# The D term of a selective scan: from the head of a batch to its second half, two products per state

## Chip, cores and metric

The kernel runs on one NeuronCore of a Trainium2 chip. The metric is the device time of one execution in microseconds (us). Its engines are TensorE (PE; PEld are its weight loads), VectorE (DVE), ScalarE (ACT), GpSimd (POOL) and SyncE (SP), which here only issues DMAs. Each engine works through its own list of instructions in order and waits on semaphores. L12 is line 12 of the kernel.

## What is computed

The whole is a two-layer block on x of 4 batches x 512 tokens x 256 features. The change touches only the state-space scan of its first layer:

```
def step(h, inp):
    dt_t, B_t, C_t, u_t = inp
    dA = jnp.exp(dt_t[:, :, None] * A)
    h = dA * h + (dt_t * u_t)[:, :, None] * B_t[:, None, :]
    y = jnp.einsum('bdn,bn->bd', h, C_t)
    return (h, y)
...
y = ys.transpose(1, 0, 2) + u2 * D
y = y * jax.nn.silu(z)
out = y @ W_out
return x + out
```

d runs over 512 channels, n over 16 states. `u2 * D` is the D term: each channel's input times one number of that channel. It doesn't depend on the state n, so it can be added to y at any point.

## The kernel before

**Stages.** Up to about 320 us the inputs of the scan are made; from there to about 655 us the scan runs; then come the rest of layer 0 and all of layer 1. The order within each engine is written by hand.

**The scan** is a loop over k = 0 to 63, with `b, n = divmod(k, 16)`: batch b, state n. Channels lie on the 128 partitions in M = 4 groups, tokens along the free axis in TILES = 4 tiles of 128. For each k:

- ACT: `times_b(k)` multiplies `duT` (dt*u2, token-major) by the state's column of B (L1716, and a scaled identity, L1717), and `decays(k, h)` makes exp(dt*A) for each half h of the channels (L1728).
- PE: `feed(k, 0)` and `feed(k, 1)` turn these products to channel-major in banks 4 to 7 of PSUM (transposes L996, one product per group L997). Half h of state k needs the scan of that half for k-1 to be done.
- DVE: `scan(k, 0)`, `scan(k, 1)` (L2133), each over 2 channel groups x 512 tokens, from PSUM into one of 7 state buffers. (The listing of instructions names their form SCALAR_TENSOR_TENSOR, the profile TENSOR_TENSOR_SCAN.)
- POOL: multiplies the state by its row of C (L2593).
- PE: `sum_state(j)`, 16 transposes (L1008) that turn the product back to token-major and add it into banks 0 to 3, one bank for each tile of tokens. It runs up to two states behind the scan: after the feeds of state k up to two sums are done, as long as `due <= k - 2`.

**The D term** (`d_term`, L950 to L959) adds u2*D into the same four banks: per tile one bf16 product of zeros, 512 wide, which opens the whole bank (L954, `nought`), and four products of a 128x128 block of `u2` with `diag`, a diagonal matrix of D (L956). In the profile each f32 product and its weight load stand as two records, a transpose as one. For batch 0 all four tiles come before the scan, ahead of the last `turn_du` (L944), which turns `du` of the batch prepared last; ACT copies that to `duT` (L1706).

**The turn of a batch.** While the first states of batch b are scanned, the result of batch b-1 leaves banks 0 to 3:

- n=1: DVE gates y (`gate_y`, L2117). n=2: PE turns it back (`turn_back`, L1016), then DVE copies two banks (L2121, signals `s_g23`) and ACT the other two (L1734, signals `s_g01`).
- n=3: PE does D of tiles 2 and 3 once `s_g23` is there, then the first output product into bank 0 (`mamba_out`, L1025), which waits for both copies. n=4: the second output product, into bank 1.
- DVE adds the products to x: `residual(b-1, 0)` between the two half scans of n=4, `residual(b-1, 1)` between those of n=5 (L2125, signals `s_x1`).
- n=5: PE waits for `s_x1`, does D of tiles 0 and 1, then the first sum of the batch. At n=2, 3 and 4 no sum was done, so at n=6, 7 and 8 it does two each.

In batch 3 DVE also has pieces of weight preparation between scans (`linear_weights`, n >= 6).

**DMA.** Batches 2 and 3 share SBUF buffers with batches 0 and 1. Their `u2`, `dt` and `duT` lie in DRAM and are loaded when free (`back`). SP also loads the rows of C for two states at a time (`c_rows_of`), issued in order. After the loop SP waits for all decays and the last D term, then loads the parameters of the next stages (`in_cond`, L723).

Of the kernel before, what the change touches and what calls it, by code (L numbers as in the profile page):

```python
# [47 lines left out]
SLOTS = 7  # L48
BIAS_ROW = 64
# [50 lines left out]
def program(nc, t_in, out):  # L100
    ctx = ExitStack()
    with ctx:
# [124 lines left out]
        one = sb("one", [P, 2])  # L227
# [413 lines left out]
        def _(sp):  # L641
# [67 lines left out]
            for j in range(B * NS // G):  # L709
                c_rows_of(j)  # L710
                b, g = divmod(j, NS // G)
                if b < 2 and g == 5:
                    back(b + 2, 0, u2[b], s_dterm, b + 1, s_back_u2)
                if 1 <= b < 3 and g == 1:
                    back(b + 1, 1, dt[b - 1], s_decay, 2 * b * NS, s_back_dt)
                    back(b + 1, 2, duT[b - 1], s_dbu, 2 * b * NS, s_back_dt)
                if 1 <= b < 3 and g == 4:
                    sp.wait_ge(s_out_mm, C * b + 1)
                    sp.dma_start(view(zT[b - 1], [[1, M * S]]), z_spill[b - 1]).then_inc(s_back_z, 16)
# [77 lines left out]
        def _(pe):  # L797
# [150 lines left out]
            nought = one[:, 1:2].bitcast(BF16)[:, 0:1]  # L948

            def d_term(b, tiles):  # L950
                if b >= 2:
                    pe.wait_ge(s_back_u2, 16 * (b - 1))
                for t in tiles:
                    pe.matmul(ps[:, t, :], nought.to_broadcast([P, P]), nought.to_broadcast([P, S]), start=True, stop=False)  # L954
                    for m in range(M):
                        last = pe.matmul(ps[:, t, m * P:(m + 1) * P], u2[b % 2][:, m, t * P:(t + 1) * P], diag[:, m, :],  # L956
                                         start=False, stop=False)
                if 0 in tiles:
                    last.then_inc(s_dterm, 1)  # L959
# [22 lines left out]
            d_term(0, range(TILES))  # L982
# [18 lines left out]
            def sum_state(k):  # L1001
                if k < B * NS - 1:
                    pe.wait_ge(s_hc, k + 1)
                else:
                    pe.wait_ge(s_ends, 2)
                for t in range(TILES):
                    for m in range(M):
                        last = pe.matmul(ps[:, t, m * P:(m + 1) * P], state[:, k % SLOTS, m, t * P:(t + 1) * P], ident,  # L1008
                                         start=False, stop=(k % NS == NS - 1 and m == M - 1), is_transpose=True)
                last.then_inc(s_y, 1)  # L1010
# [19 lines left out]
            for k in range(B * NS):  # L1030
# [3 lines left out]
                if b and n == 2:  # L1034
                    turn_back(b - 1)
                elif b and n == 3:
                    pe.wait_ge(s_g23, b)
                    d_term(b, (2, 3))
                    mamba_out(b - 1, 0, 0)
                elif b and n == 4:  # L1040
                    mamba_out(b - 1, 1, 1)
                elif b and n == 5:
                    pe.wait_ge(s_x1, C * b + 1)
                    d_term(b, (0, 1))
                    sum_state(due)
                    due += 1
                else:
                    for _ in range(2):
                        if due <= k - 2:
                            sum_state(due)  # L1050
                            due += 1
            C2, F8 = (5, 6), (7, 4)
# [936 lines left out]
        def _(dve):  # L1989
# [64 lines left out]
            dve.memset(one[:, 0:1], 1.0)  # L2054
            dve.memset(one[:, 1:2], 0.0)
# [103 lines left out]
            for k in range(B * NS):  # L2159
                b, n = divmod(k, NS)  # L2160
                scan(k, 0)
                if b and n in (4, 5):
                    residual(b - 1, n - 4)
# [570 lines left out]
```

## Time and profile before

| | us |
|---|---|
| median of 3 runs | 1590.73 (1586.46 to 1591.49) |
| the profiled execution | 1589.1 |
| its span | 1587.3 |
| PE busy | 1444.7 (91%) |
| DVE busy | 1069.1 (67%) |
| ACT busy | 854.5 (54%) |
| POOL busy | 477.4 (30%) |
| DVE L2133, 128 half scans | 284.6 busy, 40.2 idle before them |
| PE L1008, 1024 records of the sums | 121.1 busy |
| PE L956, 128 records of the D products | 18.2 busy, 9.9 idle before them |
| PE L954, the zero products | 3.7 busy |

Busy times are sums over the span. The time outside the span, 1.8 us in the profiled execution, is what lies around the program. In the timelines a row can merge instructions of one line that follow each other; the number after x says how many. The bracket at a row's end is the idle time of that engine ahead of it and who ended it.

### The profile page before, as it was taken

To read this page: it belongs to the slowest core of one execution; us is meant where nothing else is said; L and a number is where in the kernel's file an instruction comes from. 1 tells how busy PE (TensorE), PEld (TensorE's weight loads), DVE (VectorE), ACT (ScalarE), POOL (GpSimd) and SP (SyncE) were. 2 spreads that over 40 slices of the span, in tenths; PEclk is the share of its full clock that TensorE was granted. 3 is DMA by queue.
4 is the path that set the end of the run, shared out by engine and by line. 5 is a ranking of instruction groups with operands and counts; after the bars stand their busy time and mean duration, and the time that the engine had idled before them with its cause. 6 is when DMAs were issued, how large, how long until landed. Compare 5 with 4: busy or idle time off the path is not lost.

```text
span 1587.3 us, 20216 instructions
## 1 busy us (share of the span) xinstructions
PE 1444.7 (91%) x7408; PEld 985.7 (62%) x7420; DVE 1069.1 (67%) x1219; ACT 854.5 (54%) x1509; POOL 477.4 (30%) x140
## 2 busy tenths in 40 slices
PE   5898798689898999998999899999989999999997
PEld 3576343488797979753443333333358888888886
DVE  6996495789899898864443557777564565565645
ACT  3433455599899898631342267777732433333332
POOL 0999020079788888400321420000000000000000
PEclk7899999799999999978999989999999999999999
DMA  7110010502232211402112122443000000000000
GB/s 269 24 61 1 1 53 2 200 31 91 97 104 107 68 66 41 163 1 41 42 38 72 59 80 61 119 132 123 1 0 0 1 14 1 0 14 1 14 1 14
DMA packets 36624, 87.61 MB, mean 55 GB/s; under 512 B 8350, under 2 KB 24948, under 8 KB 32948
## 3 DMA queue, kind: packets, MB, share of 16 engines
q1 hardware_dynamic: 36532, 86.39, 16.3%
q8 instruction: 57, 0.93, 0.2%
q14 instruction: 35, 0.29, 0.1%
HBM read 68.10 MB, written 18.21 MB: 54 GB/s over the span
## 4 chain that ended last, share of the span: by engine, by line
PE 55%; DVE 2%; ACT 2%; issue 2%; DVEq 1%; ACTq 0%
PE ps L1440 12%; PE ps L1449 12%; PE ps L1308 4%; PE ps L1381 4%; PE ps L1175 3%; PE ps L1296 3%; PE ps L1201 2%; PE ps L1137 2%; PE ps L1008 1%; ACT arena L1909 1%; PE ps L584 1%; PE ps L1350 1%; PE ps L1059 1%; PE ps L1209 1%; PE ps L1187 1%
## 5 line engine op out<-in xcount | busy, mean ns | idle before, releaser
L2593 POOL TENSOR_TENSOR arena<-arena 128x2048 f32<-128x2048 f32 x63 | 287.4, 4591 | 158.4 <-DVE arena L2133 158.3
L2133 DVE TENSOR_TENSOR_SCAN arena<-arena,ps 128x1024 f32<-128x1024 f32 x128 | 284.6, 2272 | 40.2 <-issue 20.7
L1728 ACT ACTIVATE arena<-arena,mam 128x511 f32<-128x511 f32 x256 | 165.8, 710 | 32.0 <-DVE arena L2133 32.0
L1909 ACT ACTIVATE arena<-ps,rho 128x512 f32<-128x512 f32 x256 | 159.1, 689 | 31.4 <-PE ps L1381 30.0
L2365 DVE TENSOR_REDUCE mxs<-ps 128x1 f32<-128x512 f32 x224 | 141.2, 684 | 45.2 <-PE ps L1296 43.3
L996 PE MATMUL ps<-early,arena 128*128 128x128 f32 x768 | 130.1, 278 | 20.3 <-DVE arena L2133 15.0
L1440 PE MATMUL ps<-early,arena 128*128 128x256 f32 x512 | 127.1, 380 | 2.9 <-DVE mam L2532 1.9
L1938 ACT ACTIVATE arena<-arena 128x256 f32<-128x256 f32 x192 | 85.5, 500 | 81.5 <-DVE arena L2536 50.7
L2573 POOL TENSOR_TENSOR arena<-arena 128x4096 f32<-128x4096 f32 x16 | 115.0, 7191 | 43.5 <-DVE arena L2051 43.5
L1716 ACT ACTIVATE arena<-arena,early 128x512 f32<-128x512 f32 x192 | 123.9, 709 | 4.4 <-DVE arena L2111 4.4
L1449 PE MATMUL ps<-arena 128*128 128x256 f32 x512 | 121.0, 379 | 1.2 <-issue 1.2
L1008 PE MATMUL ps<-early,arena 128*128 128x128 f32 x1024 | 121.1, 272 | 0.9 <-POOL arena L2593 0.7
L1008 PEld LDWEIGHTS ps<-early,arena 128*128 128x128 f32 x1024 | 113.8, 140 | 1.2 <-POOL arena L2593 0.8
L996 PEld LDWEIGHTS ps<-early,arena 128*128 128x128 f32 x768 | 90.3, 142 | 35.9 <-DVE arena L2133 21.9
L1440 PEld LDWEIGHTS ps<-early,arena 128*128 128x128 f32 x512 | 96.3, 190 | 19.1 <-DVE mam L2532 3.1
L1449 PEld LDWEIGHTS ps<-arena 128*128 128x128 f32 x512 | 97.2, 190 | 14.8 <-issue 1.5
L1938 ACT ACTIVATE arena<-ps,arena 128x256 f32<-128x256 f32 x64 | 26.9, 471 | 142.6 <-PE ps L1440 142.6
L1381 PE MATMUL ps<-arena 97*128 97x512 bf16 x256 | 97.0, 389 | 6.0 <-ACT arena L1909 4.4
L997 PE MATMUL ps<-arena 128*128 128x128 f32 x512 | 99.4, 276 | 0.0
L1440 PE MATMUL ps<-arena 128*128 128x256 f32 x384 | 98.8, 380 | 0.0
L2532 DVE TENSOR_TENSOR mam<-mam,ps 128x512 f32<-128x512 f32 x32 | 22.0, 687 | 97.0 <-PE ps L1440 97.0
L1296 PE MATMUL ps<-arena 96*128 96x512 bf16 x224 | 86.6, 387 | 0.0
(352 smaller groups left out, 2482.1 us busy)
## 6 DMA issues: line engine op xcount, KB each, us to landing
arena<-bc_scratch SPq DMA_DIRECT2D x32, 512.0 KB, 3.7
arena<-in_ffn SPq DMA_DIRECT2D x8, 1024.0 KB, 5.1
batch_scratch<-arena SPq DMA_DIRECT2D x2, 3072.0 KB, 8.8
arena<-batch_scratch SPq DMA_DIRECT2D x6, 1024.0 KB, 6.9
arena<-q_scratch SPq DMA_DIRECT2D x96, 64.0 KB, 2.2
arena<-k_scratch SPq DMA_DIRECT2D x96, 64.0 KB, 2.2
arena<-in_dec_w SPq DMA_DIRECT2D x1, 3855.0 KB, 16.2
arena<-in_cond SPq DMA_DIRECT2D x1, 3739.5 KB, 11.6
```

Of the source, the lines that this page charges most:

```text
L996: pe.transpose(ps[:, FEED + m, t * P:(t + 1) * P], dub[:, k % 2, t, m * P:(m + 1) * P], ident)
L1008: last = pe.matmul(ps[:, t, m * P:(m + 1) * P], state[:, k % SLOTS, m, t * P:(t + 1) * P], ident, start=False, stop=(k % NS == NS - 1 and ...
L1296: pe.matmul(ps[:, (hg + s) % 3, :], q[0:STACK, i, qc * P:(qc + 1) * P], k[0:STACK, i, :], start=True, stop=True).then_inc(s_s_mm, 1)
L1381: pe.matmul(ps[:, 3 + (hg + n) % 3, :], k[0:STACK + 1, i, kc * P:(kc + 1) * P], q[0:STACK + 1, i, :], start=True, stop=True).then_inc(s_t_ ...
L1440: done = pe.matmul(ps[:, bank, i * S // 2:(i + 1) * S // 2], weights[:, f, :], x, start=first and i == 0, stop=last and i == 1, skip_group ...
L1449: done = pe.matmul(ps[:, bank, half * S // 2:(half + 1) * S // 2], weights[:, f, :], x[:, i, :], start=(r == 0 and half == 0 and i == 0), ...
L1716: act.activation(dub[:, k % 2, t, :], duT[b % 2][:, t, :], ACT.Copy, scale=bt[:, b, t, n:n + 1])
L1728: last = act.activation(decay[:, (2 * k + h) % 3, i, 1:S], dt[b % 2][:, m, 1:S], ACT.Exp, scale=a_neg[:, m * NS + n:m * NS + n + 1])
L1909: act.activation(pt[:, j % 4, i], ps[:, 3 + (hg + n) % 3, :], ACT.Exp, scale=rho[:, 0:1]).then_inc(s_pt, 1)
L2133: dve.tensor_tensor_scan(half, view(decay[:, (2 * k + h) % 3], [[1, 2 * S]]), view(ps[:, FEED + 2 * h, :], [[1, 2 * S]]), 0.0, ALU.mult, A ...
L2365: dve.tensor_reduce(mxs[:, hg % 2, qc, i:i + 1], ps[:, (turn + s) % 3, :], AX, ALU.max).then_inc(s_max, 1)
L2593: pool.tensor_tensor(state[:, k % SLOTS], state[:, k % SLOTS], view(c_rows[:, j % 2, k % G, :], [[0, M], [1, S]]), ALU.mult).then_inc(s_hc, 1)
```

## The change

- The zero products are gone. A bank is now begun by the first transpose of the first state's sum (`start` is set for the first group of state 0), and all that follows in it adds.
- `d_term(b, n)` is called once per state from n = 8 on (`D_FROM`), behind the sums, and does two of the 16 D products: half of a tile. Nothing of D is left before the scan, at n=3 or at n=5.
- At n=5 the first sum of a batch is split: tiles 2 and 3 run before the wait for `s_x1`, tiles 0 and 1 behind it.
- DVE does `residual(b-1, 1)` ahead of the first half scan of n=5 instead of behind it.
- SP reloads `u2` for batches 2 and 3 during batches 1 and 2 (g=2, that is n=4), instead of during batches 0 and 1 (g=5). `s_dterm`, which this reload and the load after the loop wait for, is now signalled at n=15 of each batch.

```diff
--- before.py
+++ after.py
@@ -46,6 +46,7 @@
 HG = P // SLOT
 HALF = H // 2 + 1
 SLOTS = 7
+D_FROM = NS - 2 * TILES
 BIAS_ROW = 64
 ORDER = (2, 3, 0, 1)
 
@@ -224,7 +225,7 @@
         hflat = hT[:, :, :].rearrange("p c n -> p (c n)")
         dec_b = view(hflat, [[1, D + 1]], 3 * TILES * D)
         diag = sb("diag", [P, M, P])
-        one = sb("one", [P, 2])
+        one = sb("one", [P, 1])
         at = 0
         BATCH = 3 * M * S
         u2 = [carve(b * BATCH, M, S)[0] for b in range(B)]
@@ -709,11 +710,11 @@
             for j in range(B * NS // G):
                 c_rows_of(j)
                 b, g = divmod(j, NS // G)
-                if b < 2 and g == 5:
-                    back(b + 2, 0, u2[b], s_dterm, b + 1, s_back_u2)
                 if 1 <= b < 3 and g == 1:
                     back(b + 1, 1, dt[b - 1], s_decay, 2 * b * NS, s_back_dt)
                     back(b + 1, 2, duT[b - 1], s_dbu, 2 * b * NS, s_back_dt)
+                if 1 <= b < 3 and g == 2:
+                    back(b + 1, 0, u2[b - 1], s_dterm, b, s_back_u2)
                 if 1 <= b < 3 and g == 4:
                     sp.wait_ge(s_out_mm, C * b + 1)
                     sp.dma_start(view(zT[b - 1], [[1, M * S]]), z_spill[b - 1]).then_inc(s_back_z, 16)
@@ -945,17 +946,14 @@
                                                 ident)
                     last.then_inc(s_duT_mm, 1)
 
-            nought = one[:, 1:2].bitcast(BF16)[:, 0:1]
-
-            def d_term(b, tiles):
-                if b >= 2:
+            def d_term(b, n):
+                if b >= 2 and n == D_FROM:
                     pe.wait_ge(s_back_u2, 16 * (b - 1))
-                for t in tiles:
-                    pe.matmul(ps[:, t, :], nought.to_broadcast([P, P]), nought.to_broadcast([P, S]), start=True, stop=False)
-                    for m in range(M):
-                        last = pe.matmul(ps[:, t, m * P:(m + 1) * P], u2[b % 2][:, m, t * P:(t + 1) * P], diag[:, m, :],
-                                         start=False, stop=False)
-                if 0 in tiles:
+                for m in range(M // 2 * (n % 2), M // 2 * (n % 2 + 1)):
+                    t = (n - D_FROM) // 2
+                    last = pe.matmul(ps[:, t, m * P:(m + 1) * P], u2[b % 2][:, m, t * P:(t + 1) * P], diag[:, m, :],
+                                     start=False, stop=False, skip_group_check=True)
+                if n == NS - 1:
                     last.then_inc(s_dterm, 1)
 
             pe.wait_ge(s_mam, 32)
@@ -979,7 +977,6 @@
                 else:
                     turn_du(i - 1, (6, 6))
             pe.wait_ge(s_dt, 2 * B)
-            d_term(0, range(TILES))
             pe.wait_ge(s_dbl, B + 1)
             pe.wait_ge(s_bt, B)
             turn_du(B - 1, (6, 4))
@@ -1003,11 +1000,15 @@
                     pe.wait_ge(s_hc, k + 1)
                 else:
                     pe.wait_ge(s_ends, 2)
-                for t in range(TILES):
+                sum_tiles(k, range(TILES)).then_inc(s_y, 1)
+
+            def sum_tiles(k, tiles):
+                for t in tiles:
                     for m in range(M):
                         last = pe.matmul(ps[:, t, m * P:(m + 1) * P], state[:, k % SLOTS, m, t * P:(t + 1) * P], ident,
-                                         start=False, stop=(k % NS == NS - 1 and m == M - 1), is_transpose=True)
-                last.then_inc(s_y, 1)
+                                         start=(k % NS == 0 and m == 0), stop=(k % NS == NS - 1 and m == M - 1),
+                                         is_transpose=True, skip_group_check=True)
+                return last
 
             def turn_back(b):
                 pe.wait_ge(s_yz, b + 1)
@@ -1034,21 +1035,22 @@
                 if b and n == 2:
                     turn_back(b - 1)
                 elif b and n == 3:
-                    pe.wait_ge(s_g23, b)
-                    d_term(b, (2, 3))
                     mamba_out(b - 1, 0, 0)
                 elif b and n == 4:
                     mamba_out(b - 1, 1, 1)
                 elif b and n == 5:
+                    pe.wait_ge(s_hc, due + 1)
+                    sum_tiles(due, (2, 3))
                     pe.wait_ge(s_x1, C * b + 1)
-                    d_term(b, (0, 1))
-                    sum_state(due)
+                    sum_tiles(due, (0, 1)).then_inc(s_y, 1)
                     due += 1
                 else:
                     for _ in range(2):
                         if due <= k - 2:
                             sum_state(due)
                             due += 1
+                    if n >= D_FROM:
+                        d_term(b, n)
             C2, F8 = (5, 6), (7, 4)
 
             def modulated(b):
@@ -2051,8 +2053,7 @@
                 dve.tensor_tensor(view(att_p[:, u], [[H, H], [1, H]]), view(att[:, u], [[H, H], [1, H]]),
                                   kx_row(t, [[0, H], [1, H]], RECIP), ALU.mult).then_inc(s_att, 1)
 
-            dve.memset(one[:, 0:1], 1.0)
-            dve.memset(one[:, 1:2], 0.0)
+            dve.memset(one[:, :], 1.0)
             dve.wait_ge(s_h0, B * C)
             dve.wait_ge(s_tables, 19)
             dve.wait_ge(s_mam, 16)
@@ -2158,9 +2159,11 @@
 
             for k in range(B * NS):
                 b, n = divmod(k, NS)
+                if b and n == 5:
+                    residual(b - 1, 1)
                 scan(k, 0)
-                if b and n in (4, 5):
-                    residual(b - 1, n - 4)
+                if b and n == 4:
+                    residual(b - 1, 0)
                 scan(k, 1)
                 if b and n == 1:
                     gate_y(b - 1)
```

PE before the scan (lines of the changed kernel are a few lower: L945 is the transpose L944, L993 and L994 are the feed's L996 and L997). Before:

```order
L944 MATMUL ps<-early,arena 128x128 x16
L954 MATMUL ps<-one 128x512
L956 MATMUL ps<-diag,arena 128x128 x4
L954 MATMUL ps<-one 128x512
L956 MATMUL ps<-diag,arena 128x128 x4
L954 MATMUL ps<-one 128x512
L956 MATMUL ps<-diag,arena 128x128 x4
L954 MATMUL ps<-one 128x512
L956 MATMUL ps<-diag,arena 128x128 x4
L944 MATMUL ps<-early,arena 128x128 x16
L996 MATMUL ps<-early,arena 128x128 x3
```

Now:

```order
L971 MATMUL ps<-early,arena 128x64 x4
L934 MATMUL ps<-arena,mam 128x512 x2
L945 MATMUL ps<-early,arena 128x128 x32
L993 MATMUL ps<-early,arena 128x128 x3
L994 MATMUL ps<-arena 128x128
```

The four tiles of D are gone from between the two turns of `du`, which now stand in one row of 32.

PE at n=5 of a batch, with the semaphores that are waited for. Before:

```order
L996 MATMUL ps<-early,arena 128x128 x3
L997 MATMUL ps<-arena 128x128
L954 MATMUL ps<-one 128x512 [waits x1_ready]
L956 MATMUL ps<-diag,arena 128x128 x4
L954 MATMUL ps<-one 128x512
L956 MATMUL ps<-diag,arena 128x128 x4
L1008 MATMUL ps<-early,arena 128x128 [waits state_times_c]
L1008 MATMUL ps<-early,arena 128x128 x15
```

Now:

```order
L994 MATMUL ps<-arena 128x128
L1008 MATMUL ps<-early,arena 128x128 [waits state_times_c]
L1008 MATMUL ps<-early,arena 128x128 x7
L1008 MATMUL ps<-early,arena 128x128 [waits x1_ready]
L1008 MATMUL ps<-early,arena 128x128 x7
```

Behind the feed there are no D products any more, and the wait for the residual (`x1_ready`) stands between the two halves of the sum.

DVE around n=4 and n=5 (L2133 and L2134 the half scans, L2125 and L2126 the residuals). Before:

```order
L2121 COPY hT<-ps 128x1024
L2133 SCALAR_TENSOR_TENSOR arena<-arena,ps 128x1024 x3
L2125 TENSOR_TENSOR xT<-ps,xT 128x512
L2133 SCALAR_TENSOR_TENSOR arena<-arena,ps 128x1024 x2
L2125 TENSOR_TENSOR xT<-ps,xT 128x512
L2133 SCALAR_TENSOR_TENSOR arena<-arena,ps 128x1024 x25
```

Now:

```order
L2122 COPY hT<-ps 128x1024
L2134 SCALAR_TENSOR_TENSOR arena<-arena,ps 128x1024 x3
L2126 TENSOR_TENSOR xT<-ps,xT 128x512
L2134 SCALAR_TENSOR_TENSOR arena<-arena,ps 128x1024
L2126 TENSOR_TENSOR xT<-ps,xT 128x512
L2134 SCALAR_TENSOR_TENSOR arena<-arena,ps 128x1024 x26
```

The second residual has one half scan between it and the first, not two.

PE at a state from n=8 on, now (L954 the D products, L1008 the sum):

```order
L954 MATMUL ps<-diag,arena 128x128 x2
L993 MATMUL ps<-early,arena 128x128 x3
L994 MATMUL ps<-arena 128x128
L993 MATMUL ps<-early,arena 128x128 x3
L994 MATMUL ps<-arena 128x128
L993 MATMUL ps<-early,arena 128x128 x3
L994 MATMUL ps<-arena 128x128
L993 MATMUL ps<-early,arena 128x128 x3
L994 MATMUL ps<-arena 128x128
L1008 MATMUL ps<-early,arena 128x128 x16
L954 MATMUL ps<-diag,arena 128x128 x2
```

Before, a sum was followed by the next feed directly; now two D products stand between them.

## Rows read from the trace of the kernel before

**Rows 1.** Table of stretches: window, busy us of each engine, clock, DMA share, GB/s.

```profile
405.00:487.00 82.00, 75.66 (x615) 69.59 (x618) 71.77 (x35) 71.93 (x125) 68.19 (x17) 1.00 0.26 92
```

**Rows 2.** Timeline of DVE: start, us, operation, idle before it and its releaser.

```profile
404.86 2.27 DVE L2117 TENSOR_TENSOR hT<-ps,hT 128x2048 f32<-128x2048 f32 x1
...
419.72 2.29 DVE L2133 TENSOR_TENSOR_SCAN arena<-arena,ps 128x1024 f32<-128x1024 f32 x1 [2.73 <-ACT arena L1728]
...
425.36 2.29 DVE L2133 TENSOR_TENSOR_SCAN arena<-arena,ps 128x1024 f32<-128x1024 f32 x1 [0.58 <-issue]
...
433.62 4.46 DVE L2133 TENSOR_TENSOR_SCAN arena<-arena,ps 128x1024 f32<-128x1024 f32 x2 [3.19 <-issue]
...
450.74 39.62 DVE L2133 TENSOR_TENSOR_SCAN arena<-arena,ps 128x1024 f32<-128x1024 f32 x18 [1.23 <-issue]
490.27 2.27 DVE L2117 TENSOR_TENSOR hT<-ps,hT 128x2048 f32<-128x2048 f32 x1
```

**Rows 3.** Timeline of all engines, n=3 to n=6 of batch 1, same columns.

```profile
412.73 1.00 ACT L1734 ACTIVATE hT<-ps 128x1024 f32<-128x1024 f32 x1
...
414.93 3.60 PE L1025 MATMUL ps<-hT,mam 128*128 128x512 f32 x8
...
418.36 0.49 PE L996 MATMUL ps<-early,arena 128*128 128x128 f32 x3
...
428.28 0.10 PEld L954 LDWEIGHTS ps<-one 128*128 128x128 bf16 x1 [2.11 <-DVE xT L2125]
...
430.40 1.78 PEld L1008 LDWEIGHTS ps<-early,arena 128*128 128x128 f32 x16
...
432.15 0.36 PEld L996 LDWEIGHTS ps<-early,arena 128*128 128x128 f32 x3
```

**Rows 4.** The same timeline after it, n=6 and n=7 of batch 1.

```profile
434.35 3.53 PEld L1008 LDWEIGHTS ps<-early,arena 128*128 128x128 f32 x32
...
437.85 0.36 PEld L996 LDWEIGHTS ps<-early,arena 128*128 128x128 f32 x3
```

**Rows 5.** The same timeline at the end of batch 0, ACT and PE's weight loads.

```profile
396.79 1.94 ACT L1716 ACTIVATE arena<-arena,early 128x512 f32<-128x512 f32 x3
...
400.43 0.31 PEld L996 LDWEIGHTS ps<-early,arena 128*128 128x128 f32 x3 [0.23 <-DVE arena L2133]
...
401.37 1.93 ACT L1716 ACTIVATE arena<-arena,early 128x512 f32<-128x512 f32 x3
...
403.65 0.31 PEld L996 LDWEIGHTS ps<-early,arena 128*128 128x128 f32 x3 [0.39 <-ACT arena L1717]
```

**Rows 6.** The same timeline before and at the scan's beginning.

```profile
307.20 1.97 PE L944 MATMUL ps<-early,arena 128*128 128x128 f32 x8 [4.55 <-ACT arena L1706]
...
312.06 2.02 PEld L956 LDWEIGHTS ps<-diag,arena 128*128 128x128 f32 x8
312.09 2.29 DVE L2106 TENSOR_TENSOR arena<-arena 128x2048 f32<-128x2048 f32 x1
...
316.52 0.39 ACT L1717 ACTIVATE arena<-early 128x128 f32<-128x128 f32 x1
...
317.03 1.08 PEld L956 LDWEIGHTS ps<-diag,arena 128*128 128x128 f32 x8
...
318.02 1.78 PEld L944 LDWEIGHTS ps<-early,arena 128*128 128x128 f32 x16
...
319.21 1.94 ACT L1706 ACTIVATE arena<-ps 128x1024 f32<-128x1024 f32 x2 [2.30 <-PE ps L944]
...
325.76 0.51 PEld L996 LDWEIGHTS ps<-early,arena 128*128 128x128 f32 x3 [2.33 <-ACT arena L1717]
```

**Rows 7.** Timeline at the scan's end, and issues with KB and us to landing.

```profile
649.78 0.33 SPq L723 DMA_DIRECT2D arena<-in_cond  x1
...
667.51 0.19 PEld L1090 LDWEIGHTS ps<-arena 128*128 128x128 f32 x1 [0.24 <-issue]
```

```profile
arena<-in_cond SPq DMA_DIRECT2D x1, 3739.5 KB, 11.6
```

## Prediction

> **What bounds the kernel now.** I read the table of stretches first. The scan of the four batches runs from about 322 to 655 us, and in one batch of it no engine is full: PE 75.7, DVE 71.8, ACT 71.9 of 82 us, at a granted TensorE clock of 1.00 [rows 1]. So the time lies in who waits for whom, and DVE's timeline tells it. A batch takes 85.4 us (from gating at 404.86 to the next at 490.27), of which 32 scans at 2.20 are 70.3 and the four short instructions 4.6; the other 10.5 us are gaps, all in the first half: before 419.72, before 433.62 (3.19) and before each of the next three states [rows 2]. The timeline of PE shows why: from n=3 to n=9 PE is the late engine. It works through both D parts, two output products and the arrears of sums that these left behind [rows 3, 4]. In the second half, and in all of batch 0, PE has air instead: 0.23 us before one feed half and 0.39 before the other, while ACT sets a pitch of 4.58 us a state (396.79 to 401.37) [rows 5].
>
> **The start of the scan.** Ahead of the last `turn_du`, PE now does four D tiles, 312.06 to 318.02. `du` for this turn is ready at 312.09 + 2.29 = 314.38 [rows 6]. Without the tiles the turn starts at 314.5. It may run at half clock, as the eight transposes at 307.20 did (1.97 us), so its halves end at 316.5 and 318.3. ACT is free at 316.52 + 0.39 = 316.91 and copies the halves (0.97 each) until 319.3 instead of 321.15. That is 1.8 us. ACT paces batch 0 from there on, so the gain holds to its end even if PE's first feed is slow: a cold feed half takes about 2.0 instead of 1.1 us (three loads 0.51 against 0.36 [rows 4, 6]) and delays only the first two scans. **-1.8 us, once.** (0 if ACT's copy were late anyway, -2.3 with a warm PE.)
>
> **The head of batches 1, 2 and 3.** I walk batch 1 at the old times.
> At n=3 both tiles of D go (2.15 us before the output product at 414.93). But the product needs ACT's copy too, 412.73 + 1.00 = 413.73, so it starts at 413.85: a new wait of 1.1, a gain of 1.08. The scan at 419.72, fed right behind the product (418.36 + 1.10), comes at 418.65 [rows 2, 3].
> At n=5 three things change. D's two tiles go (428.28 to 430.40, 2.12). Half of the sum runs ahead of the wait. And DVE does `residual(b-1, 1)` before its first half scan instead of behind it. The walk: DVE ends n=4 at 423.65; the second output product has ended at about 422.95; the residual runs 423.65 to 424.3, in what was the 0.58 us gap before 425.36, and the scan follows at 424.27. PE ends the feed of n=5 at 425.05, waits for nothing more, and ends the sum at 426.8. Before, it waited 2.11 us for the residual and ended the sum at 432.15 [rows 2, 3]. So PE is 5.35 ahead. Of this 0.8 is lost at once: the second feed half of n=6 needs the scan that ends at 428.7. The scans of n=6 start at 428.65 instead of 433.62 (-4.97), those of n=7 and n=8 at -4.77, still one feed (2.20: 432.15 to 434.35) and two sums (3.50: 434.35 to 437.85) apart [rows 3, 4].
>
> **The second half of each batch.** Per state from n=8 two products are added, four records. A D tile has eight records, 317.03 to 318.02, 0.99 us; so 0.50 us a state [rows 6]. All 16 products of a batch still run; only four bf16 openers a batch, 0.1 us each, vanish. At n=8 PE is still behind, so this one counts in full: -4.27 at n=9. From then on a state costs PE 2.20 + 1.75 + 0.50 = 4.45 us. In batch 0 that lies under ACT's 4.58 and in the idle 0.62: nothing. In batches 1 and 2 DVE ran at 4.39 there (39.53 us for nine states [rows 2]) on a lead that ACT had gathered while PE caught up; now PE at 4.45 and ACT at 4.58 alternate, about 4.52: 0.13 x 8 = 1.05 lost. In batch 3 DVE carries pieces of the weight work between scans and is itself slower than 4.5, so nothing is lost. **Batches 1 and 2: -3.2 each, batch 3: -4.2; -10.6 us.**
> The price of the pair is the unknown here. Lower bound 0.44 (four of sixteen transposes of a sum, 430.40 to 432.15 [rows 3]): 0.7 us better in all. Upper bound the cold tile, 312.06, 2.02 / 2 = 1.0 us [rows 6]: PE would need 4.95 a state, over ACT's 4.58, which takes 0.37 x 8 in batch 0, 0.56 x 8 in 1 and 2, and less in 3, and leaves about -1 in all. I take 0.50, since the clock there is 1.00 [rows 1].
>
> **What moves on the queues.** SP's reload of `u2` (1 MB) now stands behind the row loads of g=2 in batches 1 and 2 and waits for a D that ended some four states before; the data are wanted a whole batch later. No one waits. The parameters at the end of the scan are different: their load is issued at 649.78, five us before the last scan ends, and now also waits for the D pair of the last state, which ends some 0.9 us before that end. So it comes 4.3 later against everything else. It lands after 11.6, which was 6.1 us ahead of its first user at 667.51; 1.8 is left [rows 7]. Nothing, by a small margin; at most 2 to 3 us if it lands slower. The last pair itself (0.5) fits before the POOL-bound sum.
>
> **Sum.** -1.8 - 10.6 = -12.4 us. The profiled execution took 1589.1 (span 1587.3, 1.8 around it), so 1576.7 on that base; the median of the three runs, 1590.7, gives 1578.3. I say 1578.
>
> **The rivals.**
> (1) The products cost more between transposes than in a block. For: they have full weight loads in a stretch where PE has only 0.62 us of air. Against: each feed already changes between the two kinds four times and takes 1.10 us a half. At 0.8 us a pair the walk loses 0.17 x 8 in batch 0, 0.23 x 8 in batches 1 and 2 and 0.3 at each n=8, 5.9 together: -6.5, 1584.
> (2) The clock, ending slower. The D parts are ordinary products; without them the head of a batch and the start are nearly all transposes. The trace has a stretch where the clock fell: after the thin work of the first state the feed at 325.76 ran at half pace [rows 6]. Were PE at half clock in the PE-bound stretch from n=3 to n=9, each us of its work there would cost one more: 38 us a batch at stake, 114 in all, and the change turns slower once 12.4 us of such work (a third of one batch's head, or 4.1 a batch) run cold. With a half-cold head in one batch: +7, 1597. Against it: 32 transposes in a row at 434.35 took 3.53 at full pace [rows 4], the stretch has clock 1.00 [rows 1], and PE waits less than before.
> The Trainium skill, "TensorE: Matmul & The Clock Gate", Part 4, says that transposes do not count as busy for the clock. By that the heads would lose it, as in rival 2; the rows at 434.35 disagree with it for these f32 transposes.
> (3) The gain is given back: the order on DVE and the D removal free PE, but something not in my walk (POOL, the row loads) becomes the bound, or the start gains nothing: -4 or less, 1586.5 and up.
>
> **How the numbers follow.** Forecast (-9 to -15) 0.74; rival 1 with middle prices (-5 to -9) 0.12; rival 3 (-4.8 to +4.8) 0.09; rival 2 beyond +4.8, 0.05. 0.3% is 4.8 us, about what a measurement of this kernel can tell from no change. So faster 0.86, same 0.09, slower 0.05. Range: -6 gives 1585 at the top; at the bottom -15 and the lowest run of before, 4 under its median, meet at about 1572.
>
> **What would show it.** Right: the first scan near 320.5 or 321.5; output product of n=3 waiting for ACT about 1.1; no wait for the residual at n=5; gap before n=6 gone, those before n=7, 8 and 9 at 1.2 to 1.8; D pairs of 0.50; batches 82.2, 82.2 and the last scan 12 us earlier; the parameters used without a wait. Wrong: pairs of 0.8 or more, granted clock under 0.95 in the scan, PE waiting at the first user of the parameters, or a new idle of DVE before the moved residual.

## The result, and the profile after

The changed kernel took 1575.7 us (median of 5, 1571.4 to 1577.8) against 1586.5 for the kernel before on the same chip. The ratio is 0.9918, with a 95% interval from 0.9896 to 0.9940: 13 us less, give or take 3.5. Forecast were 12.4 us. The profiled execution has a span of 1573.9, 13.4 below before. The total agrees with the forecast, its parts do not, as the rows show.

The page of the changed kernel; the last two lines are the costliest groups, with busy time, mean ns and idle time before them:

```profile
span 1573.9 us, 20191 instructions
...
PE 1439.2 (91%) x7404; PEld 984.9 (63%) x7404; DVE 1068.6 (68%) x1218; ACT 855.6 (54%) x1509; POOL 477.6 (30%) x140
...
L2596 POOL TENSOR_TENSOR arena<-arena 128x2048 f32<-128x2048 f32 x63 | 287.6, 4584 | 150.5 <-DVE arena L2134 150.1
L2134 DVE TENSOR_TENSOR_SCAN arena<-arena,ps 128x1024 f32<-128x1024 f32 x128 | 284.4, 2272 | 32.4 <-issue 16.1
```

VectorE's idle time before its half scans fell from 40.2 to 32.4 us, and that is 7.8, not 12. The timeline of VectorE shows where:

```profile
402.82 2.27 DVE L2118 TENSOR_TENSOR hT<-ps,hT 128x2048 f32<-128x2048 f32 x1
...
418.34 2.29 DVE L2134 TENSOR_TENSOR_SCAN arena<-arena,ps 128x1024 f32<-128x1024 f32 x1 [3.39 <-ACT arena L1730]
...
423.98 8.82 DVE L2134 TENSOR_TENSOR_SCAN arena<-arena,ps 128x1024 f32<-128x1024 f32 x4
434.51 4.46 DVE L2134 TENSOR_TENSOR_SCAN arena<-arena,ps 128x1024 f32<-128x1024 f32 x2 [1.71 <-issue]
...
446.38 8.86 DVE L2134 TENSOR_TENSOR_SCAN arena<-arena,ps 128x1024 f32<-128x1024 f32 x4 [1.71 <-issue]
455.62 8.86 DVE L2134 TENSOR_TENSOR_SCAN arena<-arena,ps 128x1024 f32<-128x1024 f32 x4 [0.38 <-issue]
...
487.25 2.27 DVE L2118 TENSOR_TENSOR hT<-ps,hT 128x2048 f32<-128x2048 f32 x1
...
570.01 2.27 DVE L2118 TENSOR_TENSOR hT<-ps,hT 128x2048 f32<-128x2048 f32 x1
...
647.02 2.32 DVE L2296 TENSOR_TENSOR arena<-arena 128x2048 f32<-128x2048 f32 x1
```

I measure four distances, from the last product dt*u2 (312.09 before [rows 6], 311.62 after) to the first gate, from gate to gate, and from the third gate to the multiplication of the last state (655.01 before, 647.02 after). Their sum is called the scan stage below.

| us | before | after | difference | forecast |
|---|---|---|---|---|
| to the first gate | 92.77 | 91.20 | -1.57 | -1.8 |
| batch 1 | 85.41 | 84.43 | -0.98 | -3.2 |
| batch 2 | 85.40 | 82.76 | -2.64 | -3.2 |
| batch 3 | 79.34 | 77.01 | -2.33 | -4.2 |
| scan stage | 342.92 | 335.40 | -7.52 | -12.4 |
| ahead of it | 312.09 | 311.62 | -0.47 | 0 |
| behind it | 932.29 | 926.88 | -5.41 | 0 |

**The start** went as walked. The timeline of all engines there:

```profile
311.62 2.29 DVE L2107 TENSOR_TENSOR arena<-arena 128x2048 f32<-128x2048 f32 x1
...
314.17 3.65 PE L945 MATMUL ps<-early,arena 128*128 128x128 f32 x16 [5.46 <-DVE arena L2107]
...
317.85 1.02 ACT L1708 ACTIVATE arena<-ps 128x1024 f32<-128x1024 f32 x1 [0.50 <-PE ps L945]
...
318.93 0.90 PE L993 MATMUL ps<-early,arena 128*128 128x128 f32 x3 [1.12 <-ACT arena L1708]
...
321.44 8.82 DVE L2134 TENSOR_TENSOR_SCAN arena<-arena,ps 128x1024 f32<-128x1024 f32 x4 [7.33 <-PE ps L994]
```

TensorE turns `du` from 314.17 on, at half clock, 3.65 us for 16 where it was 1.91 in the warm; ScalarE's last copy ends at 318.87, 7.25 behind the start of `du`, where it was 9.06 ([rows 6]: 319.21 + 1.94 - 312.09). The first feed ran at half clock too (three transposes 0.90), and it cost little in the end: of the 1.8 at ScalarE's copy, 1.6 to 1.7 arrive at the first gate (the table, and e1 below).

**The head of a batch.** TensorE at n=3 and n=5 of batch 1:

```profile
411.75 5.40 PE L1026 MATMUL ps<-hT,mam 128*128 128x512 f32 x8 [0.91 <-ACT hT L1736]
...
424.72 1.79 PEld L1008 LDWEIGHTS ps<-early,arena 128*128 128x128 f32 x16
...
428.50 0.31 PEld L993 LDWEIGHTS ps<-early,arena 128*128 128x128 f32 x3 [0.84 <-DVE arena L2134]
```

and the same output product in batch 2:

```profile
496.18 3.70 PE L1026 MATMUL ps<-hT,mam 128*128 128x512 f32 x8 [0.92 <-ACT hT L1736]
```

The product waits for ScalarE's copy, 0.91 us; a wait of 1.1 was forecast. But in batch 1 it then takes 5.40 us instead of 3.60 [rows 3]. In batch 2 the same wait is followed by 3.70. The table of stretches (columns as in [rows 1]) has the granted clock of the first 3 us of each:

```profile
411.70:414.70 3.00, 2.95 (x4) 1.40 (x5) 3.00 (x2) 3.00 (x6) 2.37 (x1) 0.52 0.60 251
...
496.20:499.20 3.00, 3.00 (x7) 1.41 (x8) 3.00 (x2) 3.00 (x6) 2.30 (x1) 1.00 0.63 265
```

0.52 and 1.00: in batch 1 the product began at 1.2 GHz, in batch 2 at 2.4. Batch 3 has 5.40 again. Each such fall of the granted clock costs 1.7 us, in a stretch where TensorE is the late engine; that is the difference between 84.43 and 82.76. The wait of 2.11 us for the residual is gone (no bracket at 424.72), and at 428.50 TensorE waits for the scan instead (0.84), as walked.

**The pairs.** Weight loads of a D pair (L954), the feed behind it and the next half feed (L993):

```profile
448.86 0.52 PEld L954 LDWEIGHTS ps<-diag,arena 128*128 128x128 f32 x4
...
449.31 0.36 PEld L993 LDWEIGHTS ps<-early,arena 128*128 128x128 f32 x3
...
450.89 0.31 PEld L993 LDWEIGHTS ps<-early,arena 128*128 128x128 f32 x3 [0.40 <-DVE arena L2134]
```

The next feed follows 0.45 behind a pair's start, not 0.50. Yet two states take 9.24 us (446.38 to 455.62), 4.62 each, where 4.52 was forecast.

**The parameters.** Their load is issued at 646.21, and their first user starts at 659.51:

```profile
646.21 0.33 SPq L724 DMA_DIRECT2D arena<-in_cond  x1
...
659.51 0.19 PEld L1092 LDWEIGHTS ps<-arena 128*128 128x128 f32 x1 [0.24 <-issue]
```

In the list of issues of that stretch its landing stands:

```profile
arena<-in_cond SPq DMA_DIRECT2D x1, 3739.5 KB, 11.5
```

646.21 + 11.5 = 657.7, 1.8 us ahead of the user. The margin is the forecast one, to a tenth.

### The profile page after: what moved, and what is told of

It reads as the page before. It is cut to its first block, busy times and chain, and to the rows that moved or that the text cites. A ratio compares the mean times of both kernels' runs of the same rounds, so it can differ in the third digit from the quotient of the medians.

```text
span 1573.9 us, 20191 instructions
## 1 busy us (share of the span) xinstructions
PE 1439.2 (91%) x7404; PEld 984.9 (63%) x7404; DVE 1068.6 (68%) x1218; ACT 855.6 (54%) x1509; POOL 477.6 (30%) x140
## 4 chain that ended last, share of the span: by engine, by line
PE 71%; ACT 10%; DVE 9%; DVEq 5%; issue 3%; POOL 1%; DMA 1%; ACTq 0%; SPq 0%
PE ps L1442 12%; PE ps L1451 12%; PE ps L1008 5%; PE ps L1310 4%; PE ps L1383 4%; PE ps L1177 4%; PE ps L993 3%; ACT arena L1730 3%; DVE arena L2034 3%; ACT arena L1718 3%; PE ps L1298 2%; DVEq L2033 2%; PE ps L994 2%; PE ps L1026 2%; PE ps L1203 2%
## 5 line engine op out<-in xcount | busy, mean ns | idle before, releaser
L2134 DVE TENSOR_TENSOR_SCAN arena<-arena,ps 128x1024 f32<-128x1024 f32 x128 | 284.4, 2272 | 32.4 <-issue 16.1
L993 PE MATMUL ps<-early,arena 128*128 128x128 f32 x768 | 129.9, 278 | 15.0 <-DVE arena L2134 13.3
L1008 PE MATMUL ps<-early,arena 128*128 128x128 f32 x1024 | 121.2, 272 | 0.5 <-POOL arena L2596 0.3
L1008 PEld LDWEIGHTS ps<-early,arena 128*128 128x128 f32 x1024 | 113.8, 140 | 0.8 <-DVE arena L2296 0.4
L993 PEld LDWEIGHTS ps<-early,arena 128*128 128x128 f32 x768 | 90.9, 143 | 28.6 <-DVE arena L2134 19.1
L994 PE MATMUL ps<-arena 128*128 128x128 f32 x512 | 99.5, 276 | 0.0
## 6 DMA issues: line engine op xcount, KB each, us to landing
arena<-in_cond SPq DMA_DIRECT2D x1, 3739.5 KB, 11.5
```

Source lines behind the costliest of these rows:

```text
L993: pe.transpose(ps[:, FEED + m, t * P:(t + 1) * P], dub[:, k % 2, t, m * P:(m + 1) * P], ident)
L994: last = pe.matmul(ps[:, FEED + m, LAST:S], duT[k // NS % 2][:, TILES - 1, m * P:(m + 1) * P], dub[:, k % 2, TILES - 1, 0:P], start=True, ...
L2134: dve.tensor_tensor_scan(half, view(decay[:, (2 * k + h) % 3], [[1, 2 * S]]), view(ps[:, FEED + 2 * h, :], [[1, 2 * S]]), 0.0, ALU.mult, A ...
```

## The experiments

The scan stage and its parts, in us; "falls" counts the output products at n=3 that began at half clock (5.40 instead of 3.6 to 3.7). Ratios are to the kernel before, executed on the same chip beside each run; where none is given, the run was executed once. The stages are those of one profiled execution of each kernel.

| run | first gate | batch 1 | batch 2 | batch 3 | stage | falls | ratio (interval) |
|---|---|---|---|---|---|---|---|
| before | 92.77 | 85.41 | 85.40 | 79.34 | 342.92 | 0 | |
| after | 91.20 | 84.43 | 82.76 | 77.01 | 335.40 | 2 | 0.9918 (0.9896 to 0.9940) |
| e1_again | 91.06 | 84.42 | 82.73 | 77.02 | 335.23 | 2 | 0.9919 (0.9894 to 0.9944) |
| e2_d_moved_only | 91.05 | 85.00 | 83.35 | 75.90 | 335.30 | 1 | 0.9949 (0.9923 to 0.9974) |
| e3_residual_only | 93.35 | 83.32 | 83.34 | 77.21 | 337.22 | 0 | 0.9967 (0.9948 to 0.9986) |
| e4_d0_at_start | 92.06 | 82.70 | 82.73 | 75.32 | 332.81 | 0 | 0.9911 (0.9876 to 0.9945) |
| e5_d_left_out | 91.01 | 81.32 | 81.32 | 76.54 | 330.19 | 1 | |
| e6_d_twice | 93.16 | 84.98 | 84.98 | 76.41 | 339.53 | 0 | |
| e7_sum_in_wait | 91.03 | 82.72 | 82.75 | 75.31 | 331.81 | 0 | 0.9939 (0.9919 to 0.9960) |
| e8_filler_n3 | 91.18 | 82.73 | 82.72 | 75.31 | 331.94 | 0 | |
| e9_between | 90.97 | 81.42 | 81.43 | 77.01 | 330.83 | 1 | |
| e10_sum_earlier | 91.04 | 81.38 | 81.36 | 74.12 | 327.90 | 0 | 0.9897 (0.9875 to 0.9918) |
| e11_best | 90.98 | 79.68 | 79.69 | 74.10 | 324.45 | 0 | 0.9881 (0.9861 to 0.9902) |

**Theory.** The D products moved into idle time and the wait for the residual went, about 11 us (342.92 to 331.8 in e7 and e8, which have no fall); two falls of the clock took 3.4 of it back; the rest of the gain in the profile lies outside the scan and comes from the clock. **Rivals.** The order on VectorE alone does it; the pairs cost nothing or much; the gain behind the scan belongs to the change.

### e1: the same kernel again

> The changed kernel once more, unedited. My theory: the scan stage (from the start of the last product dt*u2 on VectorE, L2107, to the multiplication of the last state, L2296) takes about 335.4 us as in its first profile, against 342.9 before. The granted clock falls at the first output product (n=3) in some of batches 1 to 3, not always the same ones, 1.7 us each time; where it doesn't fall, a batch (gate to gate) takes 82.8, where it does, 84.4. The stretch behind the scan stage, which the change does not touch, took 932.3 us before and 926.9 after: chance, so here anywhere from 926 to 933. Rival: the shorter stretch behind the scan belongs to the change (the parameters' load or the earlier end of the scan), then it is again 927 +- 1.

The two falls came at the same products, and each batch agrees within 0.03. Behind the scan stage it again took 926.8. So the first half of my expectation held, but "anywhere from 926 to 933" was not seen here: these two profiled executions repeat each other, falls and all. That alone would speak for the rival; e4 bears on it. Two profiles don't show that every execution is alike: the six of this run took 1572.2 to 1580.1, and only one of them was profiled.

### e2: D moved, VectorE's order as before

```diff
-                if b and n == 5:
-                    residual(b - 1, 1)
                 scan(k, 0)
-                if b and n == 4:
-                    residual(b - 1, 0)
+                if b and n in (4, 5):
+                    residual(b - 1, n - 4)
```

> The changed kernel with VectorE's residual of n=5 back between the two half scans. My theory: the move of the D products alone brings most; of the scan stage's gain the order on VectorE is 1.8 us, so the stage takes about 337 us (335.4 + 1.8), and TensorE waits about 2 us for the residual at n=5. Rival: the order on VectorE is what frees TensorE, the stage goes back to 341 or more.

Each of batches 1 and 2 is 0.6 longer (84.42 to 85.00, 82.73 to 83.35), and so is batch 3 against a run without a fall (75.90 to 75.31). That is the 1.8 us expected. The stage stayed at 335.3 only because batch 3 had no fall here. The wait for the residual is there, between the two halves of the split sum:

```profile
428.42 0.85 PEld L1008 LDWEIGHTS ps<-early,arena 128*128 128x128 f32 x8 [1.28 <-DVE xT L2126]
```

It is 1.28 us on the loads, not 2: TensorE comes to the wait with half a sum already done, and 2.11 less that half (0.88) is 1.23. Without its one fall this run would stand at 333.6, 9.3 below before.

### e3: VectorE's order alone

```diff
+                if b and n == 5:
+                    residual(b - 1, 1)
                 scan(k, 0)
-                if b and n in (4, 5):
-                    residual(b - 1, n - 4)
+                if b and n == 4:
+                    residual(b - 1, 0)
```

> The kernel before with only VectorE's residual of n=5 moved ahead of the half scan; all D products where they were. My theory: 1.9 us per batch, 5.7 in all, so the scan stage takes about 337.2 us, since the wait of 2.11 us for the residual disappears. Together with e2 this would show that the two parts overlap (5.7 + 11 is more than the whole). Rival: without the D products gone, TensorE is late anyway and it brings under 2 us (341 or more).

337.22, to the digit, but partly by luck: each batch gained 2.1 (1.9 expected), and the first gate came 0.6 later (93.35 to 92.77), although nothing ahead of it was changed. The four D tiles before the scan took 6.54 there (310.92 to 317.46) instead of 5.96, because more of them ran at half clock. So a difference of 0.6 at the first gate can be the clock alone. One moved line on VectorE is worth 2.1 us a batch in the old kernel and 0.6 in the new one, where the wait that it removes is 1.28 instead of 2.11, and TensorE then waits 0.84 for the scan at n=6. With e2 this answers the rival: the order alone brings 5.7 us, the moved D products alone 9.3 without a fall, both together 11; they overlap.

### e4: batch 0's D products before the scan

```diff
             pe.wait_ge(s_dt, 2 * B)
+            d_tiles()
...
-                    if n >= D_FROM:
+                    if b and n >= D_FROM:
```

> The changed kernel with batch 0's D products all before the scan, as it was, batches 1 to 3 as changed (no zero product; each bank is begun by its own first D product). My theory: the scan stage is 1.6 to 1.8 us longer than in the changed kernel (337.1), all of it before the gate of batch 0, whose distance from the last dt*u2 goes from 91.2 back to 92.8. Rival: the cold first feed eats the gain, no difference.

Half a miss: the first gate is 1.0 later than in e1 (92.06 to 91.06), not 1.6 to 1.8. The timeline of its start:

```profile
313.55 5.32 PEld L962 LDWEIGHTS ps<-diag,arena 128*128 128x128 f32 x32 [3.29 <-DVE arena L2110]
...
318.79 1.78 PEld L945 LDWEIGHTS ps<-early,arena 128*128 128x128 f32 x16
...
319.98 1.94 ACT L1716 ACTIVATE arena<-ps 128x1024 f32<-128x1024 f32 x2 [1.57 <-PE ps L945]
```

Without the four zero products the tiles take 5.24 (313.55 to 318.79), not 5.96 [rows 6]; that is the missing 0.7. So of the 1.7 at the start, 1.0 is the move and about 0.7 the zero products (e3 shows that the clock can move this stretch by 0.6, so the split is rough). The rest of this run matters more: no output product fell, and batches 1 to 3 took 82.70, 82.73 and 75.32. That is the change without the falls: -2.7, -2.7 and -4.0.

It also bears on the stretch behind the scan. That took 932.2 us here, as before, although the parameters' load stands behind the same last D pair as in the changed kernel. The table of stretches, from the multiplication of the last state to the end, columns as in [rows 1], of before, after and this run:

```profile
655.01:1587.30 932.29, 881.54 (x3865) 551.39 (x3870) 537.95 (x817) 409.59 (x726) 62.03 (x55) 0.97 0.13 40
```

```profile
647.02:1573.90 926.88, 875.63 (x3870) 549.72 (x3870) 537.29 (x817) 409.96 (x727) 61.97 (x55) 0.98 0.13 42
```

```profile
646.40:1578.60 932.20, 881.47 (x3865) 551.42 (x3870) 537.88 (x817) 409.64 (x727) 61.93 (x55) 0.97 0.14 42
```

It is the same work (a few records are missing from some traces): VectorE is busy 538 us in each, TensorE 881.5, 875.6 and 881.5, at a granted clock of 0.97, 0.98 and 0.97. So the 5.4 us are TensorE's time for unchanged products, at a higher clock. Over all runs the stretch took 926.8 to 932.3 (e2 931.0, e3 932.2, e5 930.7, e6 930.0, e7 930.6, e8 929.1, e9 926.8, e10 931.7, e11 931.5). The change need not bring the shorter stretch with it, as e4 shows.

One thing stays open. Most ratios agree with the gain of their run's own scan stage: e2 8.1 us by the ratio and 7.6 in the stage, e3 5.2 and 5.7, e4 14 and 10.1 (with a wide interval), e7 9.7 and 11.1, e10 16.4 and 15.0, e11 18.9 and 18.5. The changed kernel stands at 13 and 7.5, in both measurements, and 7.5 lies below both intervals. So what it gains beyond the stage of the profile is hardly an accident of a single execution. Whether its other executions had fewer falls or the better clock behind the scan as well, no profile shows. The profiled execution of e4, at 1580.4, was also the slowest of its four (1571.9 to 1580.4).

### e5 and e6: no pairs, and each pair twice

e5 keeps only the pair of n=15 (`if n == NS - 1`); e6 runs the loop of a pair twice.

```diff
-                for m in range(M // 2 * (n % 2), M // 2 * (n % 2 + 1)):
+                for m in list(range(M // 2 * (n % 2), M // 2 * (n % 2 + 1))) * 2:
```

> The changed kernel without the D products of n=8 to n=14 (only the pair of n=15 is left, so the D term is nearly missing from the output). It measures what the pairs cost where they stand now. My theory: 0.45 us a pair on TensorE; batch 0 gains under 0.5 us (ScalarE paces it at 4.58 a state), batches 1 and 2 each 0.45 at n=8 and 1.4 behind it, batch 3 about 0.5: 4.5 in all, scan stage 330.8 against 335.3. Rival: the pairs lie in idle time everywhere, gain under 1.

> The changed kernel with each D pair done twice (the D term counts double in the output). My theory: TensorE then needs 2.20 + 1.75 + 0.90 = 4.85 us a state from n=8 on and paces all four batches: +2 in batch 0, +3 in 1 and 2, +1 in 3, stage about 344. Rival: there is still room, stage under 339.

Against runs without a fall: leaving the pairs out saves nothing in batch 0 (91.01), 1.41 in batches 1 and 2, and about 0.5 in batch 3 (76.54 less one fall of 1.7 against 75.31). That is 3.3 in all, where 4.5 and for batches 1 and 2 1.85 each were expected; the stage, 330.19 for 330.8, agrees only because this run had one fall where the expectation counted on two. Doubling costs 2.1, 2.25, 2.25 and 1.1, 7.7 in all, where 9 were expected; the stage is 339.5 and not 344, again also because no product fell. The timeline of VectorE in e6 shows TensorE's sum as the pitch:

```profile
448.00 4.46 DVE L2134 TENSOR_TENSOR_SCAN arena<-arena,ps 128x1024 f32<-128x1024 f32 x2 [2.13 <-issue]
452.84 4.46 DVE L2134 TENSOR_TENSOR_SCAN arena<-arena,ps 128x1024 f32<-128x1024 f32 x2 [0.38 <-issue]
```

4.84 us from state to state, the 2.20 + 1.75 + 0.90 of the walk. With single pairs TensorE has 4.40 of work and the state still takes 4.62: the sums and the pair lie behind the second feed half, and this half waits 0.40 for the scan every second state (450.89 above). TensorE can't use that wait for what is queued behind it.

### e7 and e8: the wait at n=3 filled

```diff
                 elif b and n == 3:
+                    pe.wait_ge(s_hc, due + 1)
+                    pe.wait_ge(s_g23, b)
+                    sum_tiles(due, (2, 3))
                     mamba_out(b - 1, 0, 0)
...
-                    pe.wait_ge(s_hc, due + 1)
-                    sum_tiles(due, (2, 3))
                     pe.wait_ge(s_x1, C * b + 1)
```

e8 has the added lines only; its early half sum is overwritten at n=5.

> The changed kernel with the first half of a batch's first sum (tiles 2 and 3, 0.88 us) at n=3, where TensorE now waits 1.1 us for ScalarE's copy, instead of at n=5. My theory: that wait is what makes the granted clock fall at the output product in batches 1 and 3; with it filled the product takes 3.6 to 3.7 in all batches instead of 5.4 twice, and the stage is 3.4 shorter, 331.9. The moved work itself gains nothing, because TensorE then waits longer for the scan at n=6. Rival: the clock falls for the thin work in the 5 us before the product, not for the one wait; then it still falls, stage 335.

> The changed kernel with the same 0.88 us of transposes at n=3 as pure filler (their result is overwritten; the sum at n=5 stays whole). Same expectation as for the moved half sum if the wait alone makes the clock fall: 331.9 to 332.5, output products 3.6 to 3.7 everywhere. Rival: the clock falls as in the changed kernel, 335.

331.81 and 331.94 were measured, for 331.9 expected, and no fall in six heads. TensorE in e7, batch 1:

```profile
410.80 0.85 PEld L1008 LDWEIGHTS ps<-early,arena 128*128 128x128 f32 x8
...
411.85 3.70 PE L1026 MATMUL ps<-hT,mam 128*128 128x512 f32 x8
...
424.81 0.52 PE L993 MATMUL ps<-early,arena 128*128 128x128 f32 x3 [0.55 <-DVE arena L2135]
...
426.90 0.55 PE L993 MATMUL ps<-early,arena 128*128 128x128 f32 x3 [0.79 <-DVE arena L2135]
```

Half a sum (0.85 of loads) now fills the wait; the product takes 3.70. At n=6 TensorE waits for the scan at both halves (0.55 and 0.79), so the work taken out of n=5 gains nothing, and filler does as well as real work. Over all profiles, before included: 7 of 21 first output products fell where they waited for ScalarE, none of 18 where TensorE had work up to them. (The counts are not all independent: after and e1 are one program and fell at the same two products.) e4 and e6 had the wait and no fall, so one run without a fall proves little; that four kernels with the wait filled (e7, e8, e10, e11) had none in 12 heads makes the link strong. Whether the one wait does it, or the thin work of the whole stretch, to which the filler also adds, these runs don't separate, and I can't foretell which product falls. The whole-kernel ratio of e7, 0.9939, is no better than that of the changed kernel. The 3.4 us of the stage are in the profile, but the stretch behind was 930.6 against 926.8, which hides them. In the time of the whole kernel the filled wait is not shown to gain.

### e9, e10 and e11: towards a better kernel

e9 puts the pair between the feed halves; e10 is e7 with one more whole sum at n=5; e11 has all of it.

```diff
                 feed(k, 0)
+                if n >= D_FROM:
+                    d_term(b, n)
                 feed(k, 1)
...
                     sum_tiles(due, (0, 1)).then_inc(s_y, 1)
                     due += 1
+                    sum_state(due)
+                    due += 1
```

> The changed kernel with each D pair between the two feed halves of its state, where TensorE waits 0.4 us for a half scan every second state, instead of behind the sums. My theory: behind n=9 a state costs 4.5 instead of 4.62, 1 us less in batches 1 and 2; with k output products at half clock the stage is 330.8 + 1.7 k, k from 0 to 3. Rival: a pair ahead of the second feed half makes that one late and VectorE waits; then the batches stay at 82.7 or more.

> e7 (half a sum in the wait at n=3) and one more whole sum at n=5, which is then left out of the arrears. My theory: the time that e7 could not use (TensorE waited for the scan at n=6) is now used, 1.2 a batch: stage 328.2 against 331.8 of e7, with no output product at half clock. Rival: the longer n=5 delays the feed of n=6 and nothing is gained, 331.8.

> All three: half a sum at n=3, one more sum at n=5, D pairs between the feed halves. My theory: stage 326.7, that is 8.6 less than the changed kernel's 335.3; the whole execution 5 to 9 below the changed kernel, ratio to the kernel before 0.988 +- 0.003. Rival: POOL's multiplication by C (4.54 a state) or ScalarE (4.58) now paces, stage 328 or more.

e9: 330.83, where 330.8 + 1.7 k was expected; with its one fall (k = 1) that is 1.7 better than the walk. Batches 1 and 2 take 81.4, 1.3 less than without falls before: there the pairs now cost nearly nothing (e5, without them, has 81.32). e10: 327.90, expected 328.2. e11: 324.45, which is 2.2 less than the 326.7 expected, since the moved pairs bring 1.7 a batch on top of e10 and not 1.3 or less; it is 10.8 below the changed kernel. Its VectorE in batch 1:

```profile
403.56 2.27 DVE L2121 TENSOR_TENSOR hT<-ps,hT 128x2048 f32<-128x2048 f32 x1
...
417.38 2.29 DVE L2137 TENSOR_TENSOR_SCAN arena<-arena,ps 128x1024 f32<-128x1024 f32 x1 [1.69 <-issue]
...
423.02 4.46 DVE L2137 TENSOR_TENSOR_SCAN arena<-arena,ps 128x1024 f32<-128x1024 f32 x2
427.84 4.46 DVE L2137 TENSOR_TENSOR_SCAN arena<-arena,ps 128x1024 f32<-128x1024 f32 x2 [0.36 <-issue]
433.57 4.47 DVE L2137 TENSOR_TENSOR_SCAN arena<-arena,ps 128x1024 f32<-128x1024 f32 x2 [1.27 <-issue]
439.27 41.88 DVE L2137 TENSOR_TENSOR_SCAN arena<-arena,ps 128x1024 f32<-128x1024 f32 x19 [1.23 <-issue]
```

The rows at 427.84, 433.57 and 439.27 are n=6, 7 and 8 on. The gap before n=6 is 0.36 (none in the changed kernel), before n=7 1.27 (1.71), before n=8 1.23 (1.23), and the 1.71 before n=9 is gone: from n=8 on the half scans run without a break. The whole execution is at 0.9881 (0.9861 to 0.9902), 1571.0 us against 1589.9: faster than the kernel before by 19 us, and by its median faster than the changed kernel, though the two intervals overlap and the two were not measured side by side. POOL and ScalarE were not the bound: from n=8 on a state takes 4.41 (41.88 for 19 half scans), under the 4.54 and 4.58 that the rival names; presumably on a lead that they gather in the head, where VectorE has gaps.

## Why the prediction was right, and where not

The time, 1578 in 1572 to 1585, held: 1575.7. The forecast of the whole, -12.4, stands beside -10.8 by the medians and -13 by the ratio. Point by point:

- **The start, -1.8: right in size** (-1.6 and -1.7), also that half clock would hardly matter there. About 0.7 of it are the zero products, which I had put at 0.1 us each from their weight load alone: at full clock a tile with its zero product takes 1.10 (316.92 to 318.02), two pairs 0.90, so one costs 0.2.
- **The heads, -4.27 at n=9: nearly right where the clock held.** Batch 2 stands at -4.0 there: 41.86 behind its gate (487.25 to 529.11) against 45.88 (404.86 to 450.74). Batch 3 without a fall is at -4.0 for -4.2 (e4, e7). The missing 0.25 is a slip in my own sum: TensorE 5.35 ahead, less the 0.8 of its new wait, is 4.55 at n=7 and not 4.77, and 4.05 at n=9. Batch 2 measured 4.46 at n=7 (487.25 to 517.24, against 404.86 to 439.31).
- **"The output product starts at 413.85: a new wait of 1.1": the wait was right, its price was not.** This step failed. I costed it as 1.1 us lost and put the clock into rival 2, as a loss from the missing D products over a whole head. The rows show a smaller thing: a wait of 0.9 between light work, a fall for the first half of one product, 1.7 us, in 7 of 21 cases. In the profiled run it took 3.4 us. How many ordinary products a head has does not explain it: e7 has as many as the changed kernel and no fall. The Trainium skill ("TensorE: Matmul & The Clock Gate", Part 4) says that the full clock doesn't engage for transposes, which don't count as busy in the same way. The rows here don't agree: 32 transposes in a row took 3.53 at full pace (434.35 [rows 4]), and in e8, where the filler is transposes alone, none of the three heads fell.
- **The pair, 0.50: measured 0.45.** I took half of a tile's time, and that holds part of the zero product. "About 4.52" for a state was 4.62, because the pair and the sums wait in line behind a feed half that waits for the scan. 0.3 us a batch in 1 and 2; e9 removes it.
- **The queues: right.** The parameters landed 1.8 ahead of their user, as worked out, and the reload of `u2` was waited for by no one.
- **Behind the scan I forecast nothing, and the profile has -5.4.** e4 shows 932.2 with the same load behind the same D pair. So the agreement of the total is partly luck. The scan stage gained 7.5 of 12.4; missing are 3.4 of falls, 0.25 a batch of the slip, and 0.3 of the pairs in each of batches 1 and 2. The 5.4 behind the scan, which were not in the sum either, stood in for them.

What stays open: why the clock falls in one head and not in the next, when what TensorE does ahead of it is the same. The 3 us ahead of the product, batch 1 (a fall follows) and batch 2 (none):

```profile
408.70:411.70 3.00, 1.34 (x11) 1.13 (x10) 3.00 (x3) 3.00 (x6) 2.16 (x1) 1.00 0.74 273
493.20:496.20 3.00, 1.34 (x11) 1.16 (x11) 3.00 (x3) 3.00 (x6) 2.24 (x1) 1.00 0.92 259
```

TensorE was busy 1.34 of 3 us at a granted clock of 1.00 in both. Also open is why the changed kernel gains 5 us more by its ratio than in its profiled scan stage.

## What to carry to other kernels

- Work that depends on nothing in a loop belongs where its engine has idle time, and the best place here was directly ahead of an instruction that waits, not behind it: TensorE could not use its wait for what was queued behind (e9 against the changed kernel, 1.3 us in each of batches 1 and 2).
- When an engine is freed at one point, ask at once what it waits for next, and fill that too. Here the first change left a wait of 0.9 us at n=3 and one of 0.84 at n=6; filling both gave 7.3 us more in the scan (e1 to e10), of which 3.4 was clock, seen in one profile of each.
- Compare a profiled change stage by stage. A total that fits can be two misses.

## What the runs showed of the hardware

- Where TensorE waited 0.9 us ahead of an output product, between stretches of light work, the product began at half clock in 7 of 21 cases, 1.7 us each; with transposes in that wait none of 12 did (e7, e8, e10, e11).
- 930 us of unchanged work behind the scan took 926.8 to 932.3, with TensorE busy 875.2 to 881.5 at a granted clock of 0.98 to 0.97. This is more than many a change is worth, and it can look like the change's own gain, since two profiles of one program agreed (926.9 and 926.8).
- 32 f32 transposes of 128x128 in a row took 3.53 us at full clock (434.35 [rows 4]); 16 took 3.65 on TensorE at half clock (314.17 in the changed kernel), where 16 at full clock took 1.91 (318.13 before).
